# Cross attention by two halves of the keys, with evacuations 833 and 768 columns wide, unrolled batches and an output finished in PSUM

## The chip, the cores and the metric

The kernel runs on one core of one Trainium2 chip (trn2). The metric is device time in microseconds (us) of one launch. The kernel before takes 1874.06 us, the median of three runs (1871.58 to 1874.44).

## What is computed

One transformer-like layer on x [8 batches, 64 rows, 2048], all in float32: cross attention to a context of 1601 keys, causal self attention, and a gated low-rank feed-forward. The change touches the first step alone:

```python
a = jnp.einsum('bqd,bkd->bqk', query, key)   # query = layernorm(x), key = ctx [8, 1601, 2048]
e = jax.nn.softmax(a, axis=-1)
c = jnp.einsum('bqk,bkd->bqd', e, key)
x = x + c
```

The context serves as keys and as values, so each of its 13.1 MB per batch is needed twice: transposed (the 2048 features on the partitions) for the scores, and as it lies (keys on the partitions) for the product.

## The kernel before

Float32 accuracy at a fast matmul form is had by splitting: ScalarE (ACT) writes a rounded "hi" copy (fp32r), another engine subtracts it from the source and writes the rest as "lo", and TensorE (PE) multiplies with both. In `cross_attention` every column group of the context goes through these stages, all for one batch at a time:

- SyncE (SP) loads the context. A batch's 1601 keys are three blocks of 512 keys and a tail of 65 (`NBLK`, `BLK`, `TAIL`). A block comes in four pieces of 512 features (`load_piece`, L301), the tail in one load of 65 rows of 8 KB (`load_tail`, L304). The blocks' tiles are `rows` and `xa_raw`, the tail's is `xa_raw_tail`. A piece is loaded for the next batch when the products that read it are done (`pv_done`, L328 and L350).
- PE transposes a chunk of 128 features by 512 keys into PSUM with four 128x128 transposes (L628; the tail has 16 transposes of 66 columns, L634). ACT evacuates `xa_ct_hi` (L395), VectorE (DVE) writes `xa_ct_lo` (L493), and PE adds the chunk to the scores (L656 and L657; L662 and L663 for the tail). There are four PSUM buffers (`RING` = 4), and the scores follow three places behind (`LAG` = 3).
- When a block's scores are complete, ACT and DVE make a maximum, an exponential and a factor `alpha` for what was summed before (L407 to L428, L502 to L512). PE transposes the exponentials into `xa_e_t` (L639).
- For the product, the untransposed tiles are split in units of 128 keys by 512 features: ACT writes `xa_nat_hi` (L416), GpSimd (POOL) writes `xa_nat_lo` (L372), and DVE does both for one unit in 13 (`shared`, L561 and L562). PE multiplies (L680, L681) into one of two PSUM banks `xa_ps_o`. 52 units make a batch.
- After each block DVE adds the bank to `xa_acc` in SBUF (L527, L532). At a batch's end ACT moves the lower half (L436), and DVE adds, scales and adds x (L576, L577). The result goes to memory (L337).

The order on each engine is written out by a table of places, `TRANS`, with one batch per turn: turn 0, a hardware loop over turns 1 to 6, turn 7 and a closing turn (`turns`). Self attention and the feed-forward come after and use their own buffers.

Of the kernel before, what the change touches and what calls it, by code (L numbers as in the profile page):

```python
# [11 lines left out]
P = 128  # L12
# [22 lines left out]
SHARE, SHARED = 13, (5,)

END_SHARED = 32


def transposes():  # L40

    base = [("c", 0, c) for c in range(DC)] + [("t", k) for k in range(len(TAILS))]
    base += [("c", j, c) for j in (1, 2) for c in range(DC)]
    base.insert(0, ("q", 0))
    base.insert(LAG, ("q", 1))
    base.insert(10, ("e", 2))
    base.insert(31, ("e", 0))  # L50
    base.insert(49, ("e", 1))
    return base


TRANS = transposes()
NT = len(TRANS)
assert NT % RING == 0
Q1_AT, E2_AT = TRANS.index(("q", 1)), TRANS.index(("e", 2))
SCORE_STEPS = NBLK * DC + len(TAILS)

SPANS = [(0, 0, BLK, 0, DC), (0, BLK, BLK + TAIL, 1, DC + len(TAILS)),
         (1, 0, BLK, 0, 2 * DC + len(TAILS)), (2, 0, BLK, 1, SCORE_STEPS)]


UNITS = [(j, c, k) for j in range(NBLK) for c in range(NCOL) for k in range(KT + (j == 0))]
NU = len(UNITS)
# [12 lines left out]

def nat_reuse(u):

    return NAT if NAT - 1 <= u < EIGHTS + NAT - 1 else NAT - 1


def unit_slots():

    at = [[] for _ in range(NT)]

    def spread(units, prev, lo, hi):
        for n, u in enumerate(units):
            at[int(lo + n * (hi - lo) / len(units))].append((u, prev))

    spread(range(FIRST_OF[1] + C1_NOW, FIRST_OF[2]), True, 0, 12)
    spread(range(FIRST_OF[2], NU), True, 12, 34)
    spread(range(0, FIRST_OF[1]), False, 34, 54)
    spread(range(FIRST_OF[1], FIRST_OF[1] + C1_NOW), False, 54, NT)
    return at


UNITS_AT = unit_slots()
NATURAL_AT = [[] for _ in range(NT)]
for _s in list(range(LEAD, NT)) + list(range(LEAD)):
# [5 lines left out]
STATS_AT, EXP_AT, SUM_AT = {26: 0, 43: 1, 4: 2}, {28: 0, 45: 1, 6: 2}, 9  # L110

FOLD_AT = {LAST_SLOT[NBLK - 1, c] + 2: c for c in range(NCOL)}
FINISH_AT = {LAST_SLOT[NBLK - 1, c] + 3: c for c in range(NCOL)}

X1_STATS_AT = range(20, 20 + (RT - 1) * NCOL)
STATS_OF_X_AT, NORM_AT = {11: 0, 12: 1, 13: 2, 14: 3}, range(37, 54)


def kernel_program(nc, x, ctx, w_q, w_k, w_v, w_o, a_w, b_w, wq_w, keys, out):
    x1 = nc.dram_tensor("x1_scratch", (ROWS, D), F32, kind="Internal").ap()  # L120
    with (nc.sbuf_tensor("rows", [P, RT, D], F32) as rows,
          nc.sbuf_tensor("row_bn", [P, RT, NCOL, 6], F32) as row_bn):
        cross_attention(nc, x.rearrange("b q d -> (b q) d"), ctx, x1, rows, row_bn)
# [15 lines left out]
def rsqrt_steps(dve, w, var):  # L139
# [6 lines left out]
    for _ in range(4):  # L146
        yield dve.tensor_scalar(w[:, 3:4], w[:, 0:1], w[:, 0:1], w[:, 2:3], ALU.mult, ALU.mult)
        yield dve.scalar_tensor_tensor(out=w[:, 0:1], in0=w[:, 3:4], scalar=1.5, in1=w[:, 0:1],
                                       op0=ALU.add, op1=ALU.mult)


RSQRT_LINKS = 12


def cross_attention(nc, x_rows, ctx, x1, x1_rows, row_bn):


    ctx_v = ctx[:, 0:NBLK * BLK, :].rearrange("b (j k p) (c n) -> b j c p k n", k=KT, p=P, n=512)
    stack = ExitStack()
    with stack:  # L160
        def sb(name, shape, dt=F32):
            return stack.enter_context(nc.sbuf_tensor(name, shape, dt))
# [41 lines left out]
        raw_in = [sem(f"xa_raw_in{n}") for n in range(PIECES)]  # L204
        tail_in = sem("xa_tail_in")
# [5 lines left out]
        lo_done = sem("xa_lo_done")  # L211
        s_done = sem("xa_s_done")
# [5 lines left out]
        span_read = sem("xa_span_read")  # L218
# [1348 lines left out]
```

## Time and profile before

| | |
|---|---|
| median of three runs | 1874.06 us |
| span of the profiled execution, first to last instruction | 1873.4 us |
| TensorE matmul busy | 1731.9 us (92%) |
| VectorE, ScalarE, GpSimd busy | 901.3, 762.8, 887.0 us |
| mean granted TensorE clock | 0.970 of full speed |
| HBM read | 209.92 MB |

The profiled execution is timed by its span alone, and that lies 0.7 us under the median. Busy time of TensorE counts a matmul to its modelled end, so neighbours overlap in it; the distance from one start to the next tells what a matmul occupies. In the rows below, PEld is TensorE's weight load, and SPq a line of SyncE's own queue, which issues the transfers.

### The profile page before, as it was taken

The page shows a single profiled execution, that of the slowest core. Times are in us where ns is not written, and L with a number is a line of the kernel's source. Part 1 is how long each engine was busy: PE and PEld are TensorE (multiplying, and loading weights), DVE is VectorE, ACT ScalarE, POOL GpSimd, SP SyncE. Part 2 cuts the span into 40 slices and gives each one's busy share as a digit, 9 for nine tenths or more (in the row PEclk, how much of TensorE's full clock was granted, in tenths as well). Part 3 has the DMA queues.
Part 4 walks back from the last instruction along what each step waited for, and adds up shares of the span by engine and source line. Part 5 has one row for each costly group of instructions (what it writes and reads, how often), then busy time and mean ns, then how long its engine had stood idle before and what let it go on. Part 6 is the DMA issues. An engine that isn't in the chain of part 4 may idle for free. (4 is left out here: it accounts for less than half of the span.)

```text
span 1873.4 us, 25168 instructions
## 1 busy us (share of the span) xinstructions
PE 1731.9 (92%) x8781; PEld 1400.3 (75%) x8781; DVE 901.3 (48%) x1408; ACT 762.8 (41%) x1237; POOL 887.0 (47%) x474
## 2 busy tenths in 40 slices
PE   7898999989899963999999999999999999978999
PEld 6687877878687742788788887888878788756677
DVE  6898999989998997010220301203012030135523
ACT  4687877778777732122122221221222212110321
POOL 0778777787877762234434344333333333312010
PEclk9999999999999975999999999999999999979999
DMA  9356465555546314132232322323222332311113
GB/s 315 101 192 203 143 215 157 179 168 190 184 151 203 102 67 123 47 88 90 91 89 90 90 90 90 90 90 90 86 93 71 106 92 67 102 55 48 45 68 113
DMA packets 174921, 218.87 MB, mean 117 GB/s; under 512 B 3848, under 2 KB 102152, under 8 KB 171784
## 3 DMA queue, kind: packets, MB, share of 16 engines
q1 hardware_dynamic: 174880, 218.32, 36.3%
q8 instruction: 26, 0.43, 0.1%
q14 instruction: 15, 0.12, 0.0%
HBM read 209.92 MB, written 8.39 MB: 117 GB/s over the span
## 5 line engine op out<-in xcount | busy, mean ns | idle before, releaser
L905 POOL TENSOR_TENSOR sa_w_lo<-sa_raw,sa_w_hi 128x2048 fp32r<-128x2048 f32 x80 | 367.9, 4599 | 624.7 <-ACT sa_w_hi L919 624.7
L372 POOL TENSOR_TENSOR xa_nat_lo<-xa_raw,xa_nat_hi 128x512 fp32r<-128x512 f32 x231 | 309.8, 1362 | 96.6 <-ACT xa_nat_hi L416 95.3
L1045 DVE TENSOR_TENSOR rows<-rows,sa_ps_mm 128x512 f32<-128x512 f32 x128 | 88.1, 688 | 494.0 <-PE sa_ps_mm L759 494.0
L757 PE MATMUL sa_ps_mm<-h_hi,sa_w_hi 128*128 128x512 f32 x768 | 303.9, 396 | 1.4 <-DVE h_lo L980 1.4
L758 PE MATMUL sa_ps_mm<-h_lo,sa_w_hi 128*128 128x512 f32 x768 | 300.0, 391 | 0.0
L759 PE MATMUL sa_ps_mm<-h_hi,sa_w_lo 128*128 128x512 f32 x768 | 300.0, 391 | 0.0
L493 DVE TENSOR_TENSOR xa_ct_lo<-xa_ps_t,xa_ct_hi 128x512 fp32r<-128x512 f32 (+2 forms) x408 | 269.8, 673 | 54.4 <-ACT xa_ct_hi L395 43.7
L395 ACT ACTIVATE xa_ct_hi<-xa_ps_t 128x512 fp32r<-128x512 f32 (+2 forms) x408 | 238.5, 588 | 108.1 <-PE xa_ps_t L628 101.2
L919 ACT ACTIVATE sa_w_hi<-sa_raw 128x2048 fp32r<-128x2048 f32 x80 | 153.0, 1913 | 287.1 <-PE sa_ps_mm L759 287.1
L656 PE MATMUL xa_ps_s<-xa_ct_hi,xa_q_t 128*128 128x512 f32 x384 | 185.5, 483 | 40.6 <-DVE xa_ct_lo L493 35.6
L757 PE MATMUL sa_ps_mm<-sa_w_hi,sa_o_hi 128*128 128x512 f32 x512 | 204.3, 399 | 6.9 <-ACT sa_q_t L951 4.8
L758 PE MATMUL sa_ps_mm<-sa_w_lo,sa_o_hi 128*128 128x512 f32 x512 | 203.3, 397 | 0.0
L759 PE MATMUL sa_ps_mm<-sa_w_hi,sa_o_lo 128*128 128x512 f32 x512 | 203.2, 397 | 0.0
L372 POOL TENSOR_TENSOR xa_nat_lo<-rows,xa_nat_hi 128x512 fp32r<-128x512 f32 x112 | 157.0, 1420 | 87.7 <-ACT xa_nat_hi L416 87.6
L680 PE MATMUL xa_ps_o<-xa_nat_hi,xa_e_t 128*128 128x512 f32 (+1 forms) x416 | 173.8, 418 | 14.6 <-DVE xa_nat_lo L562 7.4
L757 PEld LDWEIGHTS sa_ps_mm<-h_hi,sa_w_hi 128*128 128x128 f32 x768 | 144.9, 189 | 35.4 <-ACT sa_v_t L951 2.3
L759 PEld LDWEIGHTS sa_ps_mm<-h_hi,sa_w_lo 128*128 128x128 f32 x768 | 144.8, 189 | 30.7
L758 PEld LDWEIGHTS sa_ps_mm<-h_lo,sa_w_hi 128*128 128x128 f32 x768 | 145.0, 189 | 29.1
L681 PE MATMUL xa_ps_o<-xa_nat_lo,xa_e_t 128*128 128x512 f32 (+1 forms) x416 | 166.5, 400 | 0.0
L628 PE MATMUL xa_ps_t<-xa_ident,xa_raw 128*128 128x128 f32 x1024 | 154.3, 273 | 0.0
L628 PEld LDWEIGHTS xa_ps_t<-xa_ident,xa_raw 128*128 128x128 f32 x1024 | 126.7, 140 | 33.9 <-issue 0.2
L657 PE MATMUL xa_ps_s<-xa_ct_lo,xa_q_t 128*128 128x512 f32 x384 | 151.8, 395 | 0.0
(184 smaller groups left out, 2450.0 us busy)
## 6 DMA issues: line engine op xcount, KB each, us to landing
xa_raw<-in_ctx SPq DMA_DIRECT2D x64, 1024.0 KB, 5.0
rows<-in_ctx SPq DMA_DIRECT2D x32, 1024.0 KB, 5.6
sa_raw<-in_L_attn_w_q SPq DMA_DIRECT2D x32, 1024.0 KB, 5.8
sa_raw<-in_L_attn_w_o SPq DMA_DIRECT2D x32, 1024.0 KB, 4.9
sa_raw<-in_L_attn_w_k SPq DMA_DIRECT2D x8, 1024.0 KB, 5.1
sa_raw<-in_L_attn_w_v SPq DMA_DIRECT2D x8, 1024.0 KB, 5.0
xa_raw_tail<-in_ctx SPq DMA_DIRECT2D x8, 520.0 KB
xa_xq<-in_x SPq DMA_DIRECT2D x8, 512.0 KB, 4.8
```

Source lines behind the costliest of these rows:

```text
L372: pool.tensor_tensor(nat_lo[0:rows, nat_slot(u), :], src, nat_hi[0:rows, nat_slot(u), :].bitcast(F32), ALU.subtract).then_inc(nat_pool, 1)
L395: act.activation(ct_hi[:, bank, 0:w], ps_t[:, bank, 0:w], ACT.Copy).then_inc(hi_done, 1)
L493: dve.tensor_tensor(ct_lo[:, bank, 0:w], ps_t[:, bank, 0:w], ct_hi[:, bank, 0:w].bitcast(F32), ALU.subtract).then_inc(lo_done, 1)
L628: ins.append(pe.transpose(ps_t[:, bank, k * P:(k + 1) * P], piece(j, g // KT)[:, k, g % KT * P:(g % KT + 1) * P], ident[:]))
L656: pe.matmul(o, q_t[:, g, :], ct_hi[:, bank, :], start=g == 0, stop=False)
L680: pe.matmul(o, e_t[0:rows, j, k, :], nat_hi[0:rows, nat_slot(u), :], start=k == 0, stop=False)
L681: pe.matmul(o, e_t[0:rows, j, k, :], nat_lo[0:rows, nat_slot(u), :], start=False, stop=u == LAST_OF[j, c]).then_inc(pv_done, 1)
L757: pe.matmul(out, hi, mov_hi, start=first, stop=False)
L758: pe.matmul(out, hi, mov_lo, start=False, stop=False)
L759: return pe.matmul(out, lo, mov_hi, start=False, stop=last)
L905: pool.tensor_tensor(w_lo[:, n, :], raw[:, n, :], w_hi[:, n, :].bitcast(F32), ALU.subtract).then_inc(w_lo_done, 1)
L919: act.activation(w_hi[:, n % 2, :], raw[:, n % 2, :], ACT.Copy).then_inc(w_hi_done, 1)
```

## The change

Cross attention is written anew; the rest of the kernel is the same. What differs:

1. **Keys.** Two halves instead of three blocks and a tail: 833 keys as four tiles of 128 rows and three of 107, and 768 keys as six tiles of 128 (`TILES`). A piece of the first half (512 features) is loaded by two transfers, one of 128 x 4 x 512 and one of 107 x 3 x 512; a piece of the second half by one of 128 x 6 x 512.
2. **Steps.** One step is 128 features of a whole half: seven or six transposes, one evacuation by ACT and one by DVE (833 or 768 columns), four score matmuls (512 + 322 or 512 + 256 columns, hi and lo). A batch has 32 steps. There are two PSUM buffers of 1024 columns (`RING` = 2), and scores follow two steps behind. The transposes of the exponentials and of the queries (`SIDE`) share these steps' evacuation places.
3. **Product.** Units are pairs of tiles, 1024 columns, four pair buffers (`NAT` = 4); ACT writes hi, POOL writes lo, and DVE takes lo only for the last eight pairs of the last batch.
4. **Output.** ACT copies the first half's sums to `xa_acc`; for the second half DVE adds `alpha` times that into PSUM in place, ACT copies the lower half out, DVE folds it and finishes from PSUM, column group by column group, and each group is stored by itself.
5. **Control.** All batches are unrolled (no hardware loop, waits on constants), buffers are placed by address, the statistics of finished rows come at the very end, and the square root has three Newton steps, not four.

```diff
-NBLK = 3
-KT = 4
-BLK = KT * P
-TAIL = LK - NBLK * BLK
-RING = 4
-LAG = 3
+HALVES = 2
+TILES = [[128] * 4 + [107] * 3, [128] * 6]
+RING = 2
+LAG = 2
+NAT = 4
...
+    tile_rows = ((0, 4, 128), (4, 7, 107)), ((0, 6, 128),)
+    def keys_of(b, x, c, k0, k1, p):
+        lo = KEY0[x] + OFFS[x][k0]
+        return ctx[b, lo:lo + (k1 - k0) * p, c * 512:(c + 1) * 512].rearrange("(k p) n -> p k n", p=p)
...
-            def load_piece(b, j, c):
-                sp.dma_start(piece(j, c), ctx_v[b, j, c]).then_inc(raw_in[j * NCOL + c], 16)
-
-            def load_tail(b):
-                sp.dma_start(raw_tail[0:TAIL, :], ctx[b, NBLK * BLK:LK, :]).then_inc(tail_in, 16)
+            def load_piece(b, x, c):
+                for k0, k1, p in tile_rows[x]:
+                    sp.dma_start(raw[x][0:p, c, k0:k1, :], keys_of(b, x, c, k0, k1, p)).then_inc(raw_in[x][c], 16)
...
+            for t in range(ALL_STEPS):
...
+                for h, c in groups_before(t, 1):
+                    b, x = divmod(h, HALVES)
+                    sp.wait_ge(pv_done, uses_before(h) + GROUP_END[x][c] + 1)
+                    if b + 1 < B:
+                        load_piece(b + 1, x, c)
...
+            def rescale(b, c):
+                dve.wait_ge(pv_done, uses_before(HALVES * b + 1) + GROUP_END[1][c] + 1)
+                dve.wait_ge(first_out, NCOL * b + c + 1)
+                dve.scalar_tensor_tensor(out=group_bank(c), in0=acc[:, column(c)], scalar=alpha[:, 0:1], in1=group_bank(c),
+                                         op0=ALU.mult, op1=ALU.add).then_inc(rescaled, 1)
...
+            def transpose_step(t):
+                stage, g = divmod(t, DC)
+                b, x = divmod(stage, HALVES)
+                c = g // 4
+                if t >= RING:
+                    pe.wait_ge(lo_done, t - RING + 1)
+                if g % 4 == 0:
+                    pe.wait_ge(raw_in[x][c], 16 * len(tile_rows[x]) * (b + 1))
...
+            for t in range(ALL_STEPS):
...
+                if t % DC == 2:
+                    for h, i in USE_AT.get(t, []):
+                        product(h, i)
+                if LAG <= t < STEPS + LAG:
+                    score_step(t - LAG)
+                if t < STEPS:
+                    i = transpose_step(t)
...
+                if t % DC != 2:
+                    for h, i in USE_AT.get(t, []):
+                        product(h, i)
```

Counting the steps of batch b from 32b (first half: steps 0 to 15, second half: 16 to 31), the tables put the first half's products at steps 22 to 37, four steps to a group of 512 features, and so its last two groups into the next batch's first steps. The load of a piece is issued when its group is done: after steps 25, 29, 33 and 37. The next batch's transposes need these pieces at steps 32, 36, 40 and 44. The second half's products are at steps 38 to 52, its loads after steps 40, 44, 48 and 52, its transposes at 48, 52, 56 and 60.

On SyncE the first batch's loads are issued at the program's start. Before (`rows` is the first block, `xa_raw` the other two):

```order
L307 DMA xa_xq<-in_x 64x2048
L301 DMA rows<-in_ctx 128x4x512 x4
L304 DMA xa_raw_tail<-in_ctx 65x2048
L307 DMA xa_xq<-in_x 64x2048
L307 DMA xa_xr<-in_x 64x2048
L301 DMA xa_raw<-in_ctx 128x4x512 x8
```

Now, at the same place (`xa_raw_a` is the first half, `xa_raw_b` the second):

```order
L326 DMA xa_xq<-in_x 64x2048
L323 DMA xa_raw_a<-in_ctx 128x4x512
L323 DMA xa_raw_a<-in_ctx 107x3x512
L323 DMA xa_raw_a<-in_ctx 128x4x512
L323 DMA xa_raw_a<-in_ctx 107x3x512
L323 DMA xa_raw_a<-in_ctx 128x4x512
L323 DMA xa_raw_a<-in_ctx 107x3x512
L323 DMA xa_raw_a<-in_ctx 128x4x512
L323 DMA xa_raw_a<-in_ctx 107x3x512
L326 DMA xa_xr<-in_x 64x2048
L323 DMA xa_raw_b<-in_ctx 128x6x512 x4
```

The one load of 65 rows has become four of 107 rows, one behind each piece of the first half. In a later batch the same pairs stand, each behind a wait for the products:

```order
L323 DMA xa_raw_a<-in_ctx 128x4x512 [waits xa_pv_done]
L323 DMA xa_raw_a<-in_ctx 107x3x512
L323 DMA xa_raw_a<-in_ctx 128x4x512 [waits xa_pv_done]
L323 DMA xa_raw_a<-in_ctx 107x3x512
L323 DMA xa_raw_a<-in_ctx 128x4x512 [waits xa_pv_done]
L323 DMA xa_raw_a<-in_ctx 107x3x512
L326 DMA xa_xq<-in_x 64x2048 [waits xa_t_done]
L323 DMA xa_raw_a<-in_ctx 128x4x512 [waits xa_pv_done]
L323 DMA xa_raw_a<-in_ctx 107x3x512
L323 DMA xa_raw_b<-in_ctx 128x6x512 [waits xa_pv_done]
L357 DMA x_scratch<-xa_acc 64x512 [waits xa_finished]
```

The load of the next queries (`xa_xq`) now stands in the queue between the third and the fourth of these pairs.

On PE, two places of a batch's middle before (one unit of the product beside each chunk; `lo_done` is DVE's evacuation, `nat_pool` POOL's):

```order
L628 MATMUL xa_ps_t<-xa_ident,xa_raw 128x128 [waits xa_raw_in9,xa_lo_done]
L628 MATMUL xa_ps_t<-xa_ident,xa_raw 128x128 x3
L656 MATMUL xa_ps_s<-xa_ct_hi,xa_q_t 128x512 [waits xa_lo_done]
L657 MATMUL xa_ps_s<-xa_ct_lo,xa_q_t 128x512
L680 MATMUL xa_ps_o<-xa_nat_hi,xa_e_t 128x512 [waits xa_nat_pool]
L681 MATMUL xa_ps_o<-xa_nat_lo,xa_e_t 128x512
```

And one step of a first half now, at the place where the second piece (`raw_in01`) is first needed:

```order
L611 MATMUL xa_ps_s<-xa_ct_hi,xa_q_t 128x512 [waits xa_lo_done]
L611 MATMUL xa_ps_s<-xa_ct_hi,xa_q_t 128x322
L611 MATMUL xa_ps_s<-xa_ct_lo,xa_q_t 128x512
L611 MATMUL xa_ps_s<-xa_ct_lo,xa_q_t 128x322
L574 MATMUL xa_ps_t<-xa_ident,xa_raw_a 128x128 [waits xa_raw_in01,xa_lo_done]
L574 MATMUL xa_ps_t<-xa_ident,xa_raw_a 128x128 x3
L574 MATMUL xa_ps_t<-xa_ident,xa_raw_a 128x107 x3
L589 MATMUL xa_ps_t<-xa_ident,xa_expo 128x64 [waits xa_e_ready]
L589 MATMUL xa_ps_t<-xa_ident,xa_expo 128x64
L631 MATMUL xa_ps_o<-xa_nat_hi,xa_e_t 128x512 [waits xa_nat_pool]
L631 MATMUL xa_ps_o<-xa_nat_lo,xa_e_t 128x512
```

PE's waits are now two to a step of 13 to 15 instructions, and a transpose of the exponentials stands inside the step.

## Rows read from the trace of the kernel before

**Rows 1.** The page, part 1: busy time, share and instructions.

```profile
PE 1731.9 (92%) x8781; PEld 1400.3 (75%) x8781; DVE 901.3 (48%) x1408; ACT 762.8 (41%) x1237; POOL 887.0 (47%) x474
```

**Rows 2.** Windows; columns: stretch, its length, busy by engine, granted clock, DMA share, GB/s.

```profile
100.00:200.00 100.00, 95.28 (x581) 77.44 (x580) 92.48 (x150) 76.96 (x151) 77.39 (x58) 1.00 0.57 190
...
700.00:750.00 50.00, 16.27 (x67) 12.25 (x65) 36.53 (x68) 13.41 (x19) 10.19 (x7) 0.50 0.40 116
900.00:1000.00 100.00, 100.00 (x464) 81.67 (x463) 19.68 (x25) 22.02 (x19) 38.26 (x9) 1.00 0.29 85
```

**Rows 3.** SyncE's timeline: start, duration, what was issued.

```profile
258.11 0.51 SPq L307 DMA_DIRECT2D xa_xq<-in_x  x1
...
340.50 0.51 SPq L307 DMA_DIRECT2D xa_xq<-in_x  x1
```

**Rows 4.** PE's timeline in two places of a batch.

```profile
302.38 0.40 PE L680 MATMUL xa_ps_o<-xa_nat_hi,xa_e_t 128*128 128x512 f32 x1
302.62 0.39 PE L681 MATMUL xa_ps_o<-xa_nat_lo,xa_e_t 128*128 128x512 f32 x1
302.85 0.60 PE L628 MATMUL xa_ps_t<-xa_ident,xa_raw 128*128 128x128 f32 x4
...
303.75 0.40 PE L680 MATMUL xa_ps_o<-xa_nat_hi,xa_e_t 128*128 128x512 f32 x1
...
282.38 0.28 PE L662 MATMUL xa_ps_s<-xa_ct_hi,xa_q_t 128*128 128x66 f32 x1
...
283.72 0.66 PE L628 MATMUL xa_ps_t<-xa_ident,xa_raw 128*128 128x128 f32 x4
```

**Rows 5.** Waits, 0 to 900 us: total, times, longest.

```profile
PEld xa_ps_s L656 <- DVE xa_ct_lo L493: 49.3, 39, 3.6
...
PEld xa_ps_o L680 <- DVE xa_nat_lo L562: 16.0, 7, 4.7
```

**Rows 6.** DVE's timeline before a stall of PE.

```profile
305.36 1.65 DVE L577 SCALAR_TENSOR_TENSOR xa_res<-xa_res,xa_total,xa_xr 64x512 f32<-64x512 f32 x1
306.94 1.27 DVE L493 TENSOR_TENSOR xa_ct_lo<-xa_ps_t,xa_ct_hi 128x512 fp32r<-128x512 f32 x2
```

**Rows 7.** Groups of instructions in one batch, 258.11 to 340.5 us.

```profile
L372 POOL TENSOR_TENSOR xa_nat_lo<-xa_raw,xa_nat_hi 128x512 fp32r<-128x512 f32 x31 | 41.3, 1351 | 11.8 <-ACT xa_nat_hi L416 11.6
L493 DVE TENSOR_TENSOR xa_ct_lo<-xa_ps_t,xa_ct_hi 128x512 fp32r<-128x512 f32 x48 | 32.3, 683 | 5.4 <-ACT xa_ct_hi L395 3.8
L395 ACT ACTIVATE xa_ct_hi<-xa_ps_t 128x512 fp32r<-128x512 f32 x48 | 28.5, 595 | 12.1 <-PE xa_ps_t L628 11.6
...
L416 ACT ACTIVATE xa_nat_hi<-xa_raw 128x512 fp32r<-128x512 f32 x30 | 18.6, 626 | 0.0
...
L493 DVE TENSOR_TENSOR xa_ct_lo<-xa_ps_t,xa_ct_hi 128x330 fp32r<-128x330 f32 x2 | 0.9, 484 | 0.0
```

**Rows 8.** The page, part 6: transfers, KB each, us from issue to landing.

```profile
xa_raw<-in_ctx SPq DMA_DIRECT2D x64, 1024.0 KB, 5.0
...
xa_raw_tail<-in_ctx SPq DMA_DIRECT2D x8, 520.0 KB
xa_xq<-in_x SPq DMA_DIRECT2D x8, 512.0 KB, 4.8
```

**Rows 9.** Windows with loads under way; columns as in Rows 2.

```profile
10.00:20.00 10.00, 6.84 (x35) 6.00 (x36) 6.30 (x14) 3.01 (x6) 0.00 (x0) 1.00 0.99 318
171.60:172.60 1.00, 1.00 (x8) 0.85 (x7) 0.06 (x1) 0.24 (x1) 1.00 (x1) 1.00 0.83 197
333.50:335.50 2.00, 1.99 (x13) 1.48 (x14) 2.00 (x4) 0.58 (x2) 2.00 (x2) 1.00 1.06 416
```

**Rows 10.** First and last score, and self attention's first instruction on DVE.

```profile
17.89 0.77 PE L656 MATMUL xa_ps_s<-xa_ct_hi,xa_q_t 128*128 128x512 f32 x1
...
665.15 0.39 PE L657 MATMUL xa_ps_s<-xa_ct_lo,xa_q_t 128*128 128x512 f32 x1
...
711.85 0.26 DVE L712 BATCH_NORM_AGGREGATE sa_mv<-row_bn 128x2 f32<-128x24 f32 x1 [4.66 <-PEq L160]
```

More of the change, by code:

```diff
@@ L55 @@
[L55 to L68, printed above, removed]
@@ new lines, with pair_units, products @@
+NAT = 4
+def pair_units():
+    first = []
+    for c in range(0, NCOL, 2):
+        first += [(c, 0), (c, 2), (c, 4), (c, 6), (c + 1, 0), (c + 1, 2), (c + 1, 4)]
+    second = [(c, k) for c in range(NCOL) for k in (0, 2, 4)]
+    return [first, second]
+def products():
+    out = []
+    for x in range(HALVES):
+        units = {v: n for n, v in enumerate(PAIRS[x])}
+        uses = []
+        for c in range(NCOL):
+            both = [(c, units[c, k], [(k, 0), (k + 1, 1)]) for k in (0, 2, 4)]
+            if x == 0:
+                odd = [(c, units[c - c % 2, 6], [(6, c % 2)])]
+                both = both + odd if c % 2 == 0 else odd + both
+            uses += both
+        out.append(uses)
+    return out
@@ new lines, with evacuations, side_count, product_steps @@
+SIDE = side_transposes()
+def evacuations(t):
+    return min(t, STEPS) + 1
+def side_count(what, n, k):
+    return next(evacuations(t) for t, v in SIDE.items() if v[0] == what and v[1] == n and v[2] <= k < v[3])
+def product_steps():
+    at, step_of = {}, {}
+    for h in range(STAGES):
+        n = USES_OF[h % HALVES]
+        for i in range(n):
+            t = DC * (h + 1) + PV_AT + (i * DC // n if h < STAGES - 1 else i)
+            at.setdefault(t, []).append((h, i))
+            step_of[h, i] = t
+    return at, step_of
@@ L292, in links_per_turn, with column, uses_before, pair @@
-        def links_per_turn():
-            own = sum(shared(0, u) for u in range(NU))
-            return own + (1 + 2 + 2) + 3 + NCOL + (1 + 1 + RSQRT_LINKS)
+        def column(c):
+            return slice(c * 512, (c + 1) * 512)
+        def uses_before(h):
+            return before_half(h, USES_OF)
+        def pair(h, n):
+            x = h % HALVES
+            c, k = PAIRS[x][n]
+            if k == 6:
+                return raw[x][0:TILES[x][k], c:c + 2, k, :], TILES[x][k]
+            return raw[x][0:TILES[x][k], c, k:k + 2, :], TILES[x][k]
@@ L354, in _ @@
-            turns(sp, turn)
-            sp.wait_ge(stored, 16 * B)
+                for h, c in groups_before(t, 4):
+                    b, x = divmod(h, HALVES)
+                    if x == 1:
+                        sp.wait_ge(finished, NCOL * b + c + 1)
+                        sp.dma_start(x1[b * LQ:(b + 1) * LQ, column(c)], acc[0:LQ, column(c)]).then_inc(stored[c], 16)
+                        if c == NCOL - 1 and b + 1 < B:
+                            load_rows(b + 1, xr, xr_in)
+            for c in range(NCOL):
+                sp.wait_ge(stored[c], 16 * B)
```

788 lines of the change are left out of this document (344 added, 444 removed).

## The prediction

> **What bounds the kernel now.** I read the page's busy times first: PE is busy 92% of the span [rows 1]. Then windows, to see whether that holds in the stage that changes. In self attention PE is busy 100.00 of 100 us, in cross attention 95.28, and there DVE is busy 92.48 too [rows 2]. So the stage has two engines near full, and PE waits a little. From one load of the queries to the next, a batch takes 340.50 - 258.11 = 82.4 us [rows 3].
>
> What does PE need of that? A 512-column matmul starts 0.23 us before the next (302.62 to 302.85), and a place of four such matmuls and four 128-column transposes takes 303.75 - 302.38 = 1.37 us, so a transpose takes (1.37 - 0.92) / 4 = 0.11 us. Twelve 66-column matmuls take 283.72 - 282.38 = 1.34 us, 0.11 us each [rows 4]. A batch has 96 + 104 wide matmuls (46.0 us), 32 small ones (3.6), 192 transposes (21.1), and 45 small transposes of 64 or 66 columns, at about half of a wide one (2.5): 73 us. The other 9 us are waits and changeovers. The chain of waits names them: PE's weight loads wait 49.3 us for `xa_ct_lo` [rows 5], 6 a batch, because DVE comes late. A case: a result row of 64x512 took DVE 1.65 us, and only then, at 306.94, did `xa_ct_lo` start [rows 6].
>
> **What the engines get.** Evacuations: DVE's cost at 512 and 330 columns is 683 and 484 ns, a slope of 1.09 ns a column; so 833 columns cost 1.03 us and 768 cost 0.96. A batch's 32 take 31.9 us, against 32.3 us for 48 pieces plus 1.5 for the tail [rows 7]: 2 us less. What DVE truly loses is elsewhere: no units of the product, no accumulation of the first half, finishing from PSUM. Its load falls from about 76 us to an estimated 60 a batch. ACT has 32 evacuations (595 ns at 512; at the same slope 0.94 and 0.87 us), 26 pairs at an estimated twice 626 ns less a fixed part, 1.1 us, and smaller work, together 65 to 70 us. POOL has 26 pairs at up to twice 1351 ns: at most 70 us. All stay under PE's work, so none becomes the bound, but ACT and POOL are within 10%.
>
> PE: 160 + 48 transposes (21.9 at most), 104 wide product matmuls (23.9), 64 wide score matmuls (14.7), 32 of 322 and 32 of 256 columns. These last are in no row. They cost no less than 0.11 and no more than 0.23 us each [rows 4]; I take 0.15, as the line between the row of 66 and that of 512 columns (0.18, 0.16) lies a little high if short ones have a floor. That is 9.6 us (7.0 to 14.7). With small transposes (1.8) and more changeovers (2) the sum is 74 us (71 to 79). The Trainium skill, "TensorE: Matmul & The Clock Gate", section "Back-to-back issue gap", gives N / 2.4 + 2.5 ns for an isolated matmul: 137 and 109 ns here, which would make the sum 72; but the same formula gives 216 ns for 512 columns, and the row shows 230, so it is not used.
>
> PE's handshake. A score waits for the step's two evacuations, begun when its transposes end: about 0.94 + 1.03 us and hops of 0.1 to 0.2 each, 2.3 us. Until then PE has the product of this step, the score and transposes of the next and its product, 2.3 to 3.2 us. It fits barely, so I allow 2 us of waits a batch (0 to 6). If loads were in time, a batch would take 76 us.
>
> **The loads.** This is where I expect the time to be made. Loads today cost PE nothing: a piece lands 5.0 us after its issue [rows 8]. At full flow the 16 DMA engines show share 1.06 and 416 GB/s, 26 GB/s an engine. But the window in which only the 65-row load ran shows share 0.83 [rows 9]: 0.83 / 1.06 x 16 = 12.5, that is 13 engines, with 3 idle. And 65 = 13 x 5. It is also the one load for which the page gives no time to landing; all others have 128 or 64 rows [rows 8]. So a load is dealt out in whole rows, the same number to each engine: 8, 4 or 5. Two rules fit: the engines are the largest number up to 16 that divides the rows, or rows are dealt out in shares of ceil(rows / 16), which is 5 for 65 as well. For 107, a prime, they part: the first leaves **one** engine, the second 16. I hold to the first at about 9 in 10, as equal shares are what every load here has, and 16 shares of 107 can't be equal. The Trainium skill says the same in "DMA: Bandwidth & Descriptors", section "Why a DMA increments its semaphore by 16 and not by 1": the largest k up to 16 that divides the slowest dimension, with 127 partitions as its example of one engine. By that, the trace agrees for 65 rows (13), and for 107 no row can show it.
>
> The price: 107 x 3 rows of 2 KB are 657 KB; at 416 / 16 = 26 GB/s that takes 25.3 us, at the 318 / 16 = 19.9 GB/s of the long flow at the start 33.0 [rows 9]. I take 26, since the other 15 engines stand idle beside it. With that engine's share of the 128-row part (1 MB / 16, 2.6 us) a piece of the first half holds it for 28.6 us. Four are 114 us a batch, over PE's 76. I assume that it is the same engine each time and that its queue keeps the order of issue; no row shows either.
>
> Then a batch goes like this, from the issue of its first piece after step 25 of the batch ahead. Piece 0 lands at 30 us (28.6 and about 1.5 of start and landing); PE, which needs it at step 32, 14 us after step 25, waits. Steps 32 to 35 take 9 us, their product work frees piece 2 (step 33), issued at 35; pieces 1 and 2 have the engine until 59 and 87. Step 36 waits for 59, step 40 for 87. Piece 3, issued after step 37 at about 65, and ahead of it the queries' small share (1.3), land at 117: step 44. From there the loads are of 128 rows (4 us of that engine each) and in time: 14 steps to step 57, at 76 / 32 = 2.4 us, are 33 us; the restart costs 4. In this trace PE busy 16 us of 50 ran with a granted clock of 0.50 [rows 2], the 1.2 GHz level, and PE will now idle about 20 of each 29 us, so these bursts of 9 us may run at half clock too; three of the four are hidden by the next load, and the last is most of those 4 us. The period is 117 + 33 + 4 = **154 us**.
>
> The sum, against the profiled span of 1873.4 (0.7 under the median): first batch, piece 3 lands at about 118 (queries first, then four times 28.6), 14 steps and the restart bring step 25's end to 151. Seven periods: 1078. Steps 50 to 57 of that count, 8 x 2.4 = 19. So the last score ends at 1248, where before it is 665 [rows 10]. What follows it took 711.85 - 665.15 = 46.7 us to self attention's first instruction [rows 10]; I take 39 now: 15 us until the first product (exponential, four pair buffers at POOL's pace of 2.4 us), 12 for the last eight pairs, 3 to finish, 9 for the twelve statistics, which now come last. 1248 + 39 = 1287 against 712: +575. Forecast **2450 us**.
>
> **The rivals.**
> - *All as forecast, but the lone engine moves 19.9 GB/s*, as in the long flow. 33.0 instead of 26 us on 32 loads: +225, **2675 us**. For it: the only long stretch in the rows is that slow. Against it: there all 16 engines drew.
> - *One engine a load, but not the same one each time.* Then piece 0 still lands at 30, 16 us late; piece 2, issued at 35, lands at 65 where PE is ready at 48; pieces 1 and 3 lie beside them. Period 76 + 16 + 16 = 108, first batch +30: 1812 (below) + 7 x 32 + 30 = **2065 us**. Nothing in the rows speaks for it or against it.
> - *Faster: the 107 rows are dealt to 16 engines.* A load then lands some 8 us after issue, and PE needs it 14 us after: hidden. The change does what its compute part gives: 82.4 - 76 = 6 us a batch over 8 batches, 51, the tail 8, and nearly 2 at the start: about **1812 us** (1790 to 1855 by PE's sum of 71 to 79 and waits of 0 to 6). It decides as soon as a 107-row load lands within 14 us of its issue, which needs two engines or more. Against it stands the share of 0.83 with equal rows an engine.
>
> **How the numbers follow.** One engine, about 26 GB/s, in order: 0.80, own range 2360 to 2560 (24 to 29 us a load, 2 to 6 us of waits a batch). The slow rate: 0.06. Other engines in turn: 0.03. Hidden loads: 0.11, of which nearly all faster; 0.01 for an even result, since what can be told from no change here is about 0.2%, 4 us. The range takes in the forecast and the slow rate: 2360 to 2680. Slower 0.88, same 0.01, faster 0.11.
>
> **What the new profile would show.** Right: no time to landing, or some 27 us, for the 107 x 3 x 512 loads; long windows in the first halves with a DMA share near 1.06 / 16 = 0.07 and about 26 GB/s; PE's wait for `xa_raw_a` from a DMA as the largest of all, three or four a batch of 15 to 22 us; the queries' loads 154 us apart; a granted clock under 1 in the bursts; DVE's `xa_ct_lo` near 1.0 us. In the steps 44 to 57 PE's waits for `xa_ct_lo` should be small. Wrong: loads of 107 rows that land in 5 to 8 us; then the period of 76 us is what to look for. If PE waits mostly on ACT, DVE or POOL at a period over 82, my account of the engines failed, not that of the loads.

## The result and the profile after

The changed kernel takes **2507.9 us** (median of 4 runs, 2506.6 to 2512.3) against 1874.2 for the kernel before in the same comparison: ratio 1.339, 95% interval [1.337, 1.341]. It is slower by a third. The profiled execution took 2512.3 us, its span is 2510.5 us. It came out where the prediction had it (2450, range 2360 to 2680), 58 us above the number.

The page of the changed kernel, part 1 and the row of the granted clock (tenths of full speed, 40 slices), against [rows 1]:

```profile
PE 1792.2 (71%) x8781; PEld 1475.8 (59%) x8781; DVE 720.4 (29%) x1080; ACT 752.5 (30%) x928; POOL 855.0 (34%) x300
...
PEclk8577686876868768677695899999999999998999
```

No engine is near full: PE fell from 92 to 71% of its span, DVE from 901 to 720 us of work. The first half of the clock row, cross attention, stands at 5 to 8 in all its slices but one, the rest nearly all at 9.

The table of waits of the changed kernel, whole span (us in total, times, longest):

```profile
PE xa_ps_t L574 <- DMA xa_raw_a<-in_ctx: 565.9, 31, 35.6
...
DVE xa_bn L445 <- DMA xa_xq<-in_x: 183.5, 8, 70.8
...
PE xa_ps_s L611 <- DVE xa_ct_lo L524: 54.1, 7, 49.1
```

One line holds almost the whole loss: 31 waits of PE for the first half's keys, 566 us, where 637 us were added to the span. In before's table no wait of PE for a DMA stood, and `xa_ct_lo` led [rows 5].

PE's timeline in one batch, the starts of its transposes that waited for a DMA (start, duration, and in brackets the idle time before):

```profile
374.14 1.62 PE L574 MATMUL xa_ps_t<-xa_ident,xa_raw_a 128*128 128x128 f32 x7 [17.03 <-DMA xa_raw_a<-in_ctx]
403.52 1.62 PE L574 MATMUL xa_ps_t<-xa_ident,xa_raw_a 128*128 128x128 f32 x7 [16.73 <-DMA xa_raw_a<-in_ctx]
434.36 1.62 PE L574 MATMUL xa_ps_t<-xa_ident,xa_raw_a 128*128 128x128 f32 x7 [17.83 <-DMA xa_raw_a<-in_ctx]
465.43 1.62 PE L574 MATMUL xa_ps_t<-xa_ident,xa_raw_a 128*128 128x128 f32 x7 [20.30 <-DMA xa_raw_a<-in_ctx]
```

The four pieces come 29.4, 30.8 and 31.1 us apart. They were issued from 341.96 on, and the next batch's from 500.24: a period of 158.3 us, where it was 82.4 [rows 3].

Windows of the changed kernel in and beside those waits (columns as in [rows 2]), against [rows 2, 9]:

```profile
100.00:200.00 100.00, 47.08 (x285) 40.02 (x285) 32.87 (x51) 33.52 (x44) 26.86 (x12) 0.74 0.29 93
360.00:361.00 1.00, 0.00 (x0) 0.00 (x0) 0.00 (x0) 0.00 (x0) 0.00 (x0) 0.50 0.07 27
375.00:384.00 9.00, 9.00 (x44) 7.85 (x43) 4.21 (x6) 5.45 (x8) 4.25 (x2) 0.71 0.07 25
479.00:500.00 21.00, 19.07 (x118) 15.85 (x117) 18.39 (x24) 15.62 (x23) 14.84 (x7) 1.00 0.56 171
```

This is the signature of one DMA engine at work: a share of 0.07, which is 1.06 / 16, and 25 to 27 GB/s, while PE idles or works alike. In the nine busy microseconds behind a wait PE had a granted clock of 0.71 on average, part of them at the 1.2 GHz level; by the end of the batch it is 1.00.

Transfers of the changed kernel (KB each, us to landing), against [rows 8]:

```profile
xa_raw_b<-in_ctx SPq DMA_DIRECT2D x32, 1536.0 KB, 7.5
xa_raw_a<-in_ctx SPq DMA_DIRECT2D x32, 1024.0 KB
...
xa_raw_a<-in_ctx SPq DMA_DIRECT2D x32, 642.0 KB
...
xa_xq<-in_x SPq DMA_DIRECT2D x8, 512.0 KB, 38.6
```

The 642 KB load has no time to landing. That is no sign of one engine by itself, as the prediction had it: the 1024 KB load of 128 rows has none either. The second half's loads, of 128 rows each, move more than twice the bytes and land in 7.5 us. The queries' load, the same as before, now takes 38.6 us and not 4.8, because it stands in the queue behind the keys.

SyncE's timeline at the start (start, duration, what was issued), and two places later:

```profile
0.75 0.57 SPq L326 DMA_DIRECT2D xa_xq<-in_x  x1
1.38 85.62 SPq L323 DMA_DIRECT2D xa_raw_a<-in_ctx  x8
87.05 26.89 SPq L326 DMA_DIRECT2D xa_xr<-in_x  x1
113.97 17.57 SPq L323 DMA_DIRECT2D xa_raw_b<-in_ctx  x4
131.59 3.73 SPq L326 DMA_DIRECT2D xa_xq<-in_x  x1
183.65 22.16 SPq L323 DMA_DIRECT2D xa_raw_a<-in_ctx  x3
...
237.51 24.89 SPq L326 DMA_DIRECT2D xa_xq<-in_x  x1
...
396.50 26.45 SPq L326 DMA_DIRECT2D xa_xq<-in_x  x1
```

Here is what the prediction had not seen. SyncE itself is held while it issues: eight transfers take it 85.6 us, and one issue of the queries 25 or 26 us, where it was 0.5 [rows 3]. The queries of the second batch, which DVE needs at step 7, are therefore issued only at 131.59. DVE's first statistics on them show what that costs:

```profile
145.91 0.69 DVE L445 BATCH_NORM_STATS2 xa_bn<-xa_xq 64x6 f32<-64x512 f32 x1 [70.78 <-DMA xa_xq<-in_x]
```

`xa_ct_lo` is behind this instruction on DVE, so PE's score waits 49.06 us until 147.57: the one large wait of the third line of the table above.

Groups of one batch of the changed kernel, 341.96 to 500.27 us, against [rows 7]:

```profile
L524 DVE TENSOR_TENSOR xa_ct_lo<-xa_ps_t,xa_ct_hi 128x833 fp32r<-128x833 f32 x16 | 16.4, 1024 | 71.7 <-ACT xa_ct_hi L413 47.0 <-ACT xa_e_t L415 22.3 <-ACT xa_q_t L415 2.3
L524 DVE TENSOR_TENSOR xa_ct_lo<-xa_ps_t,xa_ct_hi 128x768 fp32r<-128x768 f32 x16 | 15.2, 951 | 9.7 <-ACT xa_ct_hi L413 5.0 <-ACT xa_q_t L415 4.7
...
L413 ACT ACTIVATE xa_ct_hi<-xa_ps_t 128x833 fp32r<-128x833 f32 x16 | 13.9, 867 | 86.4 <-PE xa_ps_t L574 64.9 <-PE xa_ps_t L589 20.4 <-PE xa_ps_t L583 1.0
L413 ACT ACTIVATE xa_ct_hi<-xa_ps_t 128x768 fp32r<-128x768 f32 x17 | 13.8, 812 | 8.7 <-PE xa_ps_t L574 5.5 <-PE xa_ps_t L583 2.3 <-PE xa_ps_t L589 0.8
```

The wide evictions cost what the slope gave: 1.02 and 0.95 us on DVE (forecast 1.03 and 0.96). ACT's are a little cheaper, 0.87 and 0.81 (0.94 and 0.87).

The last score, and self attention's first instruction with what stands ahead of it, against [rows 10]:

```profile
1304.45 0.52 PE L611 MATMUL xa_ps_s<-xa_ct_lo,xa_q_t 128*128 128x512 f32 x2
...
1342.67 7.20 DVE L558 BATCH_NORM_STATS2 row_bn<-rows 128x6 f32<-128x512 f32 x12
1350.18 0.51 DVE L659 BATCH_NORM_AGGREGATE sa_mv<-row_bn 128x2 f32<-128x24 f32 x3 [0.30 <-PEq L204]
```

From there to the end it is 1160.3 us, before 1161.6: the rest of the kernel is unchanged.

### The profile page after: what moved, and what is told of

Read it like the earlier page. It is cut to its first block and busy times, and to the rows that moved or that the text cites. A ratio compares the mean times of both kernels' runs of the same rounds, so it can differ in the third digit from the quotient of the medians.

```text
span 2510.5 us, 21640 instructions
## 1 busy us (share of the span) xinstructions
PE 1792.2 (71%) x8781; PEld 1475.8 (59%) x8781; DVE 720.4 (29%) x1080; ACT 752.5 (30%) x928; POOL 855.0 (34%) x300
## 5 line engine op out<-in xcount | busy, mean ns | idle before, releaser
L574 PE MATMUL xa_ps_t<-xa_ident,xa_raw_a 128*128 128x128 f32 (+1 forms) x896 | 146.5, 317 | 565.9 <-DMA xa_raw_a<-in_ctx 565.9
L574 PEld LDWEIGHTS xa_ps_t<-xa_ident,xa_raw_a 128*128 128x128 f32 (+1 forms) x896 | 131.4, 173 | 581.7 <-issue 575.2
L413 ACT ACTIVATE xa_ct_hi<-xa_ps_t 128x833 fp32r<-128x833 f32 (+1 forms) x256 | 214.7, 839 | 776.7 <-PE xa_ps_t L574 593.3
L524 DVE TENSOR_TENSOR xa_ct_lo<-xa_ps_t,xa_ct_hi 128x833 fp32r<-128x833 f32 (+1 forms) x256 | 252.9, 988 | 644.9 <-ACT xa_ct_hi L413 427.5
L374 POOL TENSOR_TENSOR xa_nat_lo<-xa_raw_a,xa_nat_hi 128x1024 fp32r<-128x1024 f32 (+1 forms) x112 | 267.2, 2405 | 364.8 <-ACT xa_nat_hi L388 364.8
L374 POOL TENSOR_TENSOR xa_nat_lo<-xa_raw_b,xa_nat_hi 128x1024 fp32r<-128x1024 f32 x88 | 209.4, 2384 | 478.7 <-ACT xa_nat_hi L388 478.4
L631 PE MATMUL xa_ps_o<-xa_nat_hi,xa_e_t 128*128 128x512 f32 (+1 forms) x416 | 202.2, 486 | 8.7 <-POOL xa_nat_lo L374 4.6
L611 PE MATMUL xa_ps_s<-xa_ct_hi,xa_q_t 128*128 128x512 f32 (+2 forms) x512 | 153.0, 382 | 70.1 <-DVE xa_ct_lo L524 54.1
L631 PE MATMUL xa_ps_o<-xa_nat_lo,xa_e_t 128*128 128x512 f32 (+1 forms) x416 | 181.0, 435 | 0.0
L611 PEld LDWEIGHTS xa_ps_s<-xa_ct_hi,xa_q_t 128*128 128x128 f32 x512 | 99.7, 208 | 100.7 <-DVE xa_ct_lo L524 53.1
## 6 DMA issues: line engine op xcount, KB each, us to landing
xa_xq<-in_x SPq DMA_DIRECT2D x8, 512.0 KB, 38.6
```

The lines of the kernel that those rows point to most:

```text
L374: pool.tensor_tensor(nat_lo[0:p, u % NAT, :, :], src, nat_hi[0:p, u % NAT, :, :].bitcast(F32), ALU.subtract).then_inc(nat_pool, 1)
L413: i = act.activation(ct_hi[:, t % RING, 0:w], ps_t[:, t % RING, 0:w], ACT.Copy)
L524: i = dve.tensor_tensor(ct_lo[:, t % RING, 0:w], ps_t[:, t % RING, 0:w], ct_hi[:, t % RING, 0:w].bitcast(F32), ALU.subtract)
L574: i = pe.transpose(ps_t[:, t % RING, OFFS[x][k]:OFFS[x][k] + p], raw[x][0:p, c, k, g % 4 * P:(g % 4 + 1) * P], ident[0:p, 0:p])
L611: i = pe.matmul(ps_s[:, lo:hi], q_t[:, g, :], ct[:, t % RING, lo:hi], start=g == 0 and ct is ct_hi, stop=g == DC - 1 and ct is ct_lo)
L631: ins = pe.matmul(group_bank(c), e_t[0:p, x, k, :], nat[0:p, u % NAT, half, :], start=first and (k, half) == tiles[0] and nat is nat_hi, s ...
```

## The experiments

Two theories stood against each other. The **load theory**: the 107-row transfers run on one DMA engine, and all of the loss is theirs. The **structure theory**: two wide halves are themselves slower, through their evictions or their handshake, and the loads only show where PE stops. All times below are medians, of 4 or 5 runs, with the ratio to the kernel before in the same comparison. The code cuts leave out the outer indentation and the counts that PE waits for, which follow the number of transfers.

### Cutting the 107-row loads

```
+CUTS = {107: [(0, 96), (96, 107)]}
...
 def load_piece(b, x, c):
     for k0, k1, p in tile_rows[x]:
-        sp.dma_start(raw[x][0:p, c, k0:k1, :], keys_of(b, x, c, k0, k1, p)).then_inc(raw_in[x][c], 16)
+        src = keys_of(b, x, c, k0, k1, p)
+        for lo, hi in CUTS.get(p, [(0, p)]):
+            sp.dma_start(raw[x][lo:hi, c, k0:k1, :], src[lo:hi]).then_inc(raw_in[x][c], 16)
```

> Each 107-row key load is cut into one transfer of 96 rows and one of 11; everything else is the changed kernel. Theory (the 107-row load falls on one DMA engine and its delay holds the batches): the four waits of about 18 us in each batch go, a batch takes 74 to 79 us and not 158, the first batch loses most of its 33 us excess, and the time is about 1812 us (1790 to 1855). Rival (the two-half structure is itself slower, through its evictions or its matmuls of 322 columns, and the loads only come on top): TensorE's waits move to the VectorE's or ScalarE's evictions, a batch takes 83 us or more, and the time is 1874 us or above.

Measured: **1856.1 us**, ratio 0.991 [0.989, 0.993]. This kernel's table of waits from 0 to 694 us has one wait left for the keys, that of the start; its windows and SyncE's timeline:

```profile
PE xa_ps_s L614 <- DVE xa_ct_lo L527: 23.1, 9, 16.8
PE xa_ps_t L577 <- DMA xa_raw_a<-in_ctx: 12.3, 1, 12.3
```

```profile
100.00:500.00 400.00, 388.04 (x2400) 332.82 (x2398) 274.97 (x415) 314.43 (x430) 318.73 (x135) 1.00 0.62 189
```

```profile
35.16 4.39 SPq L329 DMA_DIRECT2D xa_xq<-in_x  x1
...
191.70 0.49 SPq L329 DMA_DIRECT2D xa_xq<-in_x  x1
270.05 0.49 SPq L329 DMA_DIRECT2D xa_xq<-in_x  x1
```

The same bytes, tiles, matmuls and evictions, and 652 us less. The structure theory falls: with its loads in time the new structure takes 78.35 us a batch and the kernel is 0.9% faster than before. But the time is 44 us above the 1812 that I had given for this case, just above its range (1855); where they lie is told below. The third batch's queries and all later ones are issued in 0.5 us again.

### Another row count: 65 in place of 107

```
-TILES = [[128] * 4 + [107] * 3, [128] * 6]
+TILES = [[128] * 6 + [65], [128] * 6]
...
-    tile_rows = ((0, 4, 128), (4, 7, 107)), ((0, 6, 128),)
+    tile_rows = ((0, 6, 128), (6, 7, 65)), ((0, 6, 128),)
```

> The long half's seven tiles are six of 128 rows and one of 65, as in the kernel before, in place of four of 128 and three of 107; the halves, steps and evictions stay. Theory: the 65-row load runs on 13 engines as it did before, so no wait on the keys is left; about the time of the kernel whose 107-row loads are cut (1790 to 1855 us), within 0.5% of it, since both have the same columns and evictions. Rival (what costs is not the row count but the number of bytes the loads move in one half's time): still over 2300 us.

Measured: **1856.4 us**, ratio 0.991 [0.989, 0.993], the same as with the cut loads. No load had to be cut; a row count with the divisor 13 was enough.

### 106 rows and one: two engines

Against the kernel with the loads cut in 96 and 11:

```
-CUTS = {107: [(0, 96), (96, 107)]}
+CUTS = {107: [(0, 106), (106, 107)]}
```

> Each 107-row key load is cut into one transfer of 106 rows and one of a single row. Theory (the rows of a load are spread over the largest number of engines up to 16 that divides them, 106 = 2 x 53 giving two engines): each piece takes 26/2 = 13 us on its slowest engine plus some 2.7 us of the other rows' share, four pieces 63 to 67 us, which is less than a batch's 76 us for one half but is needed for the long half only while the short half's pieces take little; with the spacing of the four waits at some 16 to 17 us and not 30, a period of 158 - 4 x 14 = 102 us and a time of about 2040 us (1950 to 2090). First rival (any row count that isn't a multiple of 16 falls on one engine): 2490 to 2520 us. Second rival (only a count that is odd does, an even one uses all 16): about 1812 us.

Measured: **2119.9 us**, ratio 1.132 [1.130, 1.134]. A window of this kernel in a wait, and the waits of one period, 286.8 to 397.05 us:

```profile
262.00:263.00 1.00, 0.00 (x0) 0.00 (x0) 0.00 (x0) 0.00 (x0) 0.20 (x1) 0.54 0.13 49
```

```profile
PE xa_ps_t L577 <- DMA xa_raw_a<-in_ctx: 22.5, 4, 9.4
```

Share 0.13 and 49 GB/s are twice the 0.07 and 25 to 27 of one engine: two engines, as the largest divisor of 106 up to 16 gives. Both rivals fall (one engine would be 2500 us, sixteen 1812). The time missed its range by 30 us, in the main since the period is 110.25 us and not 102, which makes 58 us in seven periods. The pieces come at first 16.5 us apart, as worked out, but then 18.5 and 20.35 us; why the last ones stretch I have not separated.

### 53, 53 and one: the same engine or the next?

Again against the kernel with the loads cut in 96 and 11:

```
-CUTS = {107: [(0, 96), (96, 107)]}
+CUTS = {107: [(0, 53), (53, 106), (106, 107)]}
```

> The changed kernel with each 107-row load cut into 53, 53 and 1 rows. 53 is a prime, so each of the two large transfers should have one engine. Theory A (a one-engine transfer always takes the same engine, as the forecast assumed): the engine still carries all 107 rows of every load, and the time stays at 2500 to 2520 us. Theory B (the two follow one another on different engines): as with 106 rows on two engines, 2120 us (2080 to 2160). Which of the two holds also says whether the waits of about 30 us from piece to piece are one engine's queue.

Measured: **2503.7 us**, ratio 1.336 [1.333, 1.338]. Theory A holds: two transfers of 53 rows, a prime, go to the same engine one after the other, and nothing is gained by issuing more transfers. The prediction had assumed this without a row for it. The Trainium skill, "DMA: Bandwidth & Descriptors", section "Why a DMA increments its semaphore by 16 and not by 1", says that a hardware-queue transfer with k engines takes the lowest-numbered k. By that, this run agrees in so far as the engine is the same each time; which one it is, no run here shows. The nearly even spacings of the waits, 29.4 to 31.1 us, fit as well.

### The queries' load ahead of the keys

```
-for c in range(NCOL):
-    load_piece(0, 0, c)
+load_piece(0, 0, 0)
+load_piece(0, 0, 1)
+sp.wait_ge(first_q_done, 1)
+load_rows(1, xq, xq_in)
+load_piece(0, 0, 2)
+load_piece(0, 0, 3)
 load_rows(0, xr, xr_in)
...
-if t == 5:
-    sp.wait_ge(first_q_done, 1)
-    load_rows(1, xq, xq_in)
```

Once on the changed kernel as it is, once on top of the cut loads:

> The changed kernel with its 107-row loads as they are; only the load of the second batch's query rows is issued after the first two pieces of the first batch's keys and not at step 5, behind all eight pieces. Theory (the first batch's excess over its forecast, 184 us and not 151, is SyncE's issue of the second batch's queries held up behind the key loads, for which VectorE waits 70.8 us and TensorE 49 us): the first batch ends 20 to 33 us earlier and the time is 2475 to 2490 us. Rival (the first batch is bound by the one engine's key rows in any case, and the queries' delay lay beside them): 2500 to 2512 us, no difference.

> Both repairs together: the 107-row loads cut in 96 and 11 rows, and the second batch's query rows loaded behind two pieces of keys and not eight. Theory (of the 44 us by which the version with cut loads, 1856 us, missed my 1812, about 14 lie in the first batch: TensorE waits 12.3 us for the first piece and 16.8 us at step 7, because SyncE issues the second batch's queries only at 35.2 us): the wait of 16.8 us goes, and the time is 1840 to 1844 us. Rival (VectorE's statistics for the queries then fall elsewhere in the first batch, or the later pieces of keys come late instead): 1850 to 1856 us.

Measured: **2486.6 us**, ratio 1.327 [1.325, 1.329], 21 us less than the changed kernel; and **1840.0 us**, ratio 0.982 [0.981, 0.983], 16 us less than with the cut loads alone. Both theories hold. In the first of the two kernels the first batch ends at 160.50 us and not at 183.65. SyncE's timeline of the second has the queries issued at 17.28 instead of 35.16, and those of the third batch at 96.24 instead of 113.34:

```profile
17.28 0.48 SPq L329 DMA_DIRECT2D xa_xq<-in_x  x1
96.24 0.47 SPq L329 DMA_DIRECT2D xa_xq<-in_x  x1
```

### The wide eviction undone

```
-i = act.activation(ct_hi[:, t % RING, 0:w], ps_t[:, t % RING, 0:w], ACT.Copy)
+act.activation(ct_hi[:, t % RING, 0:512], ps_t[:, t % RING, 0:512], ACT.Copy).then_inc(hi_first, 1)
+i = act.activation(ct_hi[:, t % RING, 512:w], ps_t[:, t % RING, 512:w], ACT.Copy)
```

and the same on DVE, which waits for `hi_first` ahead of its first part.

> The version with cut loads, in which each step's wide eviction is undone: 512 columns and the rest apart, on ScalarE and on VectorE, which starts on its first part when ScalarE has written it. From the rows at 512 and 833 columns an instruction's fixed part is about 0.13 us on VectorE and 0.17 on ScalarE, so 4 and 5 us of load a batch are added. Theory (TensorE is the bound of a batch of 78.3 us with 2 us of waits, VectorE and ScalarE have spare time, and the handshake gets no longer because the two engines overlap): within 0.4% of the version with cut loads, 1850 to 1864 us. Rival (the wide eviction is where the gain of the new structure comes from): the batch goes back to 82 us and the time to 1880 us or more.

Measured: **1858.5 us**, ratio 0.992 [0.990, 0.993], 2.4 us above the kernel with one wide eviction, in the range of the theory. One wide eviction a step is worth some 0.3 us a batch. So it is not where the new structure's 4 us a batch come from.

### The same fault in the kernel before

```
-sp.dma_start(raw_tail[0:TAIL, :], ctx[b, NBLK * BLK:LK, :]).then_inc(tail_in, 16)
+for lo, hi in ((0, 61), (61, TAIL)):
+    sp.dma_start(raw_tail[lo:hi, :], ctx[b, NBLK * BLK + lo:NBLK * BLK + hi, :]).then_inc(tail_in, 16)
```

> The kernel before, with its 65-row load of the tail cut into one of 61 rows (a prime, so one DMA engine) and one of 4. Theory: the 500 KB take one engine about 20.7 us at the 24.1 GB/s that the changed kernel shows; the tail is issued 29 us before TensorE needs it (249.26 and 278.55 us in the trace of before) and the first block behind it 23 us before (258.93 and 282.02), so it stays hidden: no change, within 0.3%. Rival (a one-engine load is felt whatever its size, because SyncE and the other loads queue behind it): 1890 us or more, up to 20 us a batch, 2030 us.

Measured: **1939.5 us**, ratio 1.035 [1.033, 1.036]. My expectation was wrong. The rival's range (1890 to 2030 us) has the number, and half of its reason: a load waits in the queue behind the tail, but SyncE is not held by it, for it issues the queries in 0.51 us as before. The waits of this kernel, and its queries' transfer:

```profile
DVE xa_bn L465 <- DMA xa_xq<-in_x: 68.6, 8, 17.6
```

```profile
xa_xq<-in_x SPq DMA_DIRECT2D x8, 512.0 KB, 19.6
```

The tail itself was hidden, and so were the key blocks behind it: PE waits for neither. I had looked at these two and overlooked the small load between them, the queries, for which DVE has only 12.3 us (issued at 258.11, read at 270.42 in the trace of before). With 37 rows on the one engine:

> The kernel before with its tail cut in 37 and 28 rows (one engine with 303 KB, and 14). With 61 rows on one engine the kernel took 1939 us and not the 1873 expected: the queries' load, issued 9 us behind the tail, landed after 19.6 us and not 4.8, and VectorE needs it 12.3 us after its issue (258.11 and 270.42 in the trace of before); I had left it out. Theory: the engine is free (61 - 37) x 8 KB / 24.1 = 8 us earlier, the queries land about 11.5 us after their issue, just in time, and the time is back at 1872 to 1882 us. Rival (the loss goes by the number of bytes on the one engine, without such a limit: 37/61 of 66 us): 1913 us (1900 to 1925).

Measured: **1903.1 us**, ratio 1.016 [1.014, 1.018]. My theory (1872 to 1882 us) fell again. The time lies in the rival's range (1900 to 1925 us), 10 us under its number. The same lines of this kernel:

```profile
DVE xa_bn L465 <- DMA xa_xq<-in_x: 29.2, 8, 11.6
```

```profile
xa_xq<-in_x SPq DMA_DIRECT2D x8, 512.0 KB, 14.5
```

DVE's wait for the queries was 5.7 us in before. It grew by 62.9 and 23.5 us, and the spans of the profiled executions (1938.8, 1892.7, before 1873.4) by 65.4 and 19.3. With 37 rows that execution was the fastest of five; by the medians the loss is 29.8 us. In proportion to the bytes it would be 38 us of waits and 40 of time, so the rival's rule is too high, by 10 us in the time and 14 in the waits. The queries land 14.5 us after issue, not 11.5: the 24.1 GB/s that I took from waits in which the engine worked alone were too fast for a stretch with all 16 under way. So a one-engine load in this place costs roughly what it delays the most urgent load in its queue past its need; its own cover does not tell.

### The statistics moved into DVE's gap

The cut loads and early queries, and eight of the twelve statistics for self attention behind the last batch's row total:

```
 if g == TOTAL_AT and h > 0 and h % HALVES == 1:
     row_total(h // HALVES)
+    if h == STAGES - 1:
+        x1_stats(0)
+        x1_stats(1)
...
 if t == ALL_STEPS - 1:
-    dve.wait_ge(rows_in, 16 * (RT - 1))
-    for r in range(RT - 1):
-        for c in range(NCOL):
-            dve.bn_stats(row_bn[:, r, c, :], x1_rows[:, r, column(c)])
+    x1_stats(2)
```

> The version with cut loads and early queries, with 8 of the 12 row statistics for self attention moved from the end of cross attention to the place behind the last batch's row total, where VectorE sat idle for 4.5 us. Theory (the tail of 43 us ends in 7.2 us of statistics on VectorE, which nothing hides): 4.8 us move into the gap, of which 3 to 5 us show: 1836 to 1841 us where the version without is 1840 to 1844. Rival (the rows of x1 have not landed there and VectorE's key pairs come later by as much): no difference or up to 3 us slower.

Measured: **1833.9 us** (1832.6 to 1837.8), ratio **0.978 [0.977, 0.980]**: the fastest kernel of this study, 2.2% under the kernel before, and 2 us below the range of the theory (1836 to 1841). `x1_stats(r)` makes the four statistics of the rows of load r, behind a wait for that load alone. DVE's timeline of this kernel:

```profile
641.56 4.85 DVE L521 BATCH_NORM_STATS2 row_bn<-rows 128x6 f32<-128x512 f32 x8
...
671.54 2.46 DVE L521 BATCH_NORM_STATS2 row_bn<-rows 128x6 f32<-128x512 f32 x4
674.43 0.51 DVE L668 BATCH_NORM_AGGREGATE sa_mv<-row_bn 128x2 f32<-128x24 f32 x3 [0.43 <-PEq L205]
```

4.85 us of statistics moved into the gap, and self attention starts 41.0 us after the last score (633.39), where it was 43.2 without the move (634.10 and 677.31). That is 2.2 us; the medians differ by 6.2. The profiled execution was the slowest of the five, 1837.8, so it doesn't show the rest, and what the move is worth stays open between 1.4 us (the two spans) and 6.

## Why the prediction was right, and where its sums were off

**One engine for 107 rows.** Right, and shown: one engine's share and rate in the windows, two with 106 rows, none of it left with 96 and 11 or with 65. The assumption of the same engine each time, for which no row of before spoke, is shown by the 53-row run. The rivals "another engine each time" (2065) and "hidden" (1812) did not come, nor did the slow rate of 19.9 GB/s (2675).

**The size of a piece.** 28.6 us forecast, 29.4 to 31.1 measured: (657 + 65.5) KB in 29.4 us are 24.6 GB/s, not 26. The forecast's own terms are 25.3 + 2.6 = 27.9 us; it had put 26 us in place of 25.3. Over 32 pieces that slip is 22 us, and it brought the number nearer by luck. The first piece reached PE 32.2 us after its issue (341.96 to 374.14; forecast 30). Piece 3 reached PE 123.5 us after the first issue (341.96 to 465.43; forecast 117). From there to the next batch's issue were 34.8 us (forecast 33 + 4). Together 158.3 and not 154: 7 x 4.3 = 30 us of the miss. PE's idle was 17 to 20 us of each piece, and the bursts fell in part to the lower clock, both as told.

**The first batch**, the step that failed: 151 forecast, 183.65 measured. The 151 is also a wrong sum: 118, 33 and the restart of 4 us, which the period has, are 155. I had let the engine's own work end the batch and taken SyncE's issue as free. It isn't when the queue is full, and the queries' load stood behind eight transfers. That wait is worth 23 us in the first batch, as the trace of its repair shows (160.50 us in place of 183.65), and 21 us by the medians. The remaining 9.5 us to the forecast are the slower pieces: in that trace piece 3 reached PE at 129.51 us and not at 118, and 31 us followed it.

**The tail** was 45.7 us, not 39 (1304.45 to 1350.18). The products ended 35 us after the last score and not 27; the finish took 3.2 us and the statistics 7.5, where 3 and 9 stood. The timeline shows what held the products: POOL's pairs came one by one, PE waited two times 2 us for a finished column on DVE, and between 1316 and 1325.3 us its granted clock was 0.50, the 1.2 GHz level:

```profile
1316.00:1325.30 9.30, 7.73 (x17) 5.14 (x17) 8.78 (x5) 3.61 (x5) 5.67 (x3) 0.50 0.01 2
```

**The sum.** From 1248 to 1304.45 for the last score: +33 for the first batch, +30 for seven periods, -6 for the last steps. +6.7 for the tail, -1.3 for the rest: 62 us, and the span is 2510.5 where the sum gave 2449. With 27.9 us a piece and 155 us for the first batch the forecast's own terms give some 2430 us: still in the range, but 78 us and not 58 under the measured time.

**The structure by itself** was judged too kindly. The rival of 1812 us was built from 51 us for eight batches, 8 for the tail and 2 at the start. The cut loads show 8 x (82.4 - 78.35) = 32, then 3.5 (43.2 after 46.7), and at the start a loss of 18.5 us and no gain. PE's work a batch is 388.04 / 400 x 78.35 = 76.0 us, not 74, and it idles 2.3, as forecast (2). The sum has a slip here: 208 transposes at 0.11 us are 22.9 us and not "21.9 at most". Where the other 1 us lies is not separated. For the loss at the start, 17 us are again the queries' load behind the keys, by its repair. What was right is that no engine but PE bounds a batch: ACT is busy 79% and POOL 80% of it, DVE 69%. Their loads, 62, 62 and 54 us a batch, came out under the estimates (65 to 70, at most 70, and 60).

## What to carry to other kernels

Before a tile's row count changes, factor it: in the loads tried here the engines were the largest divisor of the rows up to 16 (13 for 65, two for 106, one for 107, 61 and 53), and one engine moved some 25 GB/s. A load's cover is not only its own distance to its use: every later load in the same queue can wait with it, and SyncE too once the queue is full, so look for the small urgent load behind the large one. Then time the structure with the loads repaired before judging it: here it was a third slower as written and 2.2% faster with three small edits.

## What the hardware showed that I had not expected

- **A full queue holds the engine that issues.** One issue by SyncE took 0.5 us before and 25 to 26 us here, eight at the start 85.6 us. With 96 and 11 rows the queries' issue is 0.5 us again from the third batch on. With 53, 53 and 1 rows it is 0.5 us too, but then twelve issues of keys take 80.4 us: which issue is held changes with what stands ahead of it. That a full queue is what holds it is a reading of these times; no row shows the queue's fill. Fast loads do it as well: with 96 and 11 rows four issues of the second half take 17.2 us at the start.
- **More transfers are not more engines.** Three transfers of 53, 53 and 1 rows took 2503.7 us, two of 106 and 1 rows 2119.9, two of 96 and 11 rows 1856.1.
- **An engine's rate is not one number.** The lone engine moved 24.6 GB/s in the changed kernel, with rows of 2 KB. In the kernel with the 61-row tail, with rows of 8 KB, it moved 29 GB/s alone; six microseconds later, with all 16 busy, they moved 239 GB/s together, 15 an engine:

```profile
292.00:296.00 4.00, 4.00 (x28) 3.13 (x27) 2.49 (x5) 2.27 (x6) 3.15 (x3) 1.00 0.07 29
298.00:302.00 4.00, 4.00 (x26) 3.37 (x25) 3.90 (x7) 3.09 (x7) 4.00 (x4) 1.00 1.02 239
```

What the engine with the tail moved in such company no row shows. From the issue of the tail at 287.2 us to DVE's first read of the queries at 315.4 it moved an estimated 600 KB (500 KB of the tail, and its shares of 65 and 33 KB of the loads beside it), some 21 GB/s with start and landing counted in.
